# Decoder block with a routed feed-forward: the rows of the routed tiles turned by way of DRAM and VectorE in place of TensorE

## What is computed

```
x = x + ffn(layernorm(x))
probs  = softmax(h @ gate_w.T)            # h = layernorm(x), 2048 x 512
w, sel = top_k(probs, 2); w = w / sum(w)  # two of 8 experts for a token
out    = silu(h @ Gs.T) * (h @ Us.T) @ Ds.T                    # shared, 704 wide
out   += sum over chosen e: w_e * (silu(h @ G_e.T) * (h @ U_e.T)) @ D_e.T   # 352 wide
```

## Time and profile before

| | |
|---|---|
| median of 3 runs | 1596.42 us (1595.49 to 1596.97) |
| the profiled execution | 1598.12 us, of which 1596.4 us is its span |
| PE busy | 1563.7 us (98%) |
| DVE busy | 1030.9 us (65%) |
| ACT busy | 584.1 us (37%) |
| POOL busy | 448.0 us (28%) |
| TensorE clock granted | 0.997 of full speed on average |
| moved by DMA | 345.37 MB, mean 216 GB/s |

### The profile page before, as it was taken

One profiled execution on the slowest core, in us unless ns is written; L12 is line 12 of the kernel. 1 busy time (PEld: TensorE's weight loads), 2 busy tenths in 40 slices (PEclk: granted clock), 3 DMA queues, 4 the chain that ended last, 5 costly groups with the idle time before them and its releaser, 6 DMA issues.

```text
span 1596.4 us, 24261 instructions
## 1 busy us (share of the span) xinstructions
PE 1563.7 (98%) x8012; PEld 1352.6 (85%) x8013; DVE 1030.9 (65%) x2219; ACT 584.1 (37%) x997; POOL 448.0 (28%) x378
## 2 busy tenths in 40 slices
PE   7999999999999999999999999999999999999996
PEld 5888888888888888888888887788999989999995
DVE  4798767788777788777787778655663582222221
ACT  4454443434434334434334334333111312333332
POOL 3445332234123234222233221102200003333342
PEclk9999999999999999999999999999999999999998
DMA  8886564677676786776686776564621026778753
GB/s 290 282 305 211 184 219 146 237 279 260 256 268 226 261 303 238 257 282 224 243 312 248 297 303 241 165 209 157 239 94 54 7 105 211 235 201 267 211 87 40
DMA packets 97601, 345.37 MB, mean 216 GB/s; under 512 B 10144, under 2 KB 24992, under 8 KB 92000
## 3 DMA queue, kind: packets, MB, share of 16 engines
q1 hardware_dynamic: 84480, 306.33, 52.7%
q0 software_dynamic: 13024, 37.79, 10.1%
HBM read 224.03 MB, written 120.05 MB: 216 GB/s over the span
## 4 chain that ended last, share of the span: by engine, by line
PE 90%; DVE 5%; DMA 2%; POOL 1%; issue 1%; ACT 1%; SPq 0%; POOLq 0%; DVEq 0%; ACTq 0%
PE bank L360 29%; PE bank L362 28%; PE bank L361 28%; PE bank L1912 1%; PE bank L2029 1%; DMA wqk_raw<-wqk_in 1%; DMA wqk<-wqk_parts 1%; POOL store L633 0%; DVE resid L1235 0%; PE bank L1702 0%; DMA wv_raw<-wv_in 0%; DMA rows<-x_rows,ids_e 0%; POOL wqk L633 0%; PE bank L1986 0%; DVE place_hot L1591 0%
## 5 line engine op out<-in xcount | busy, mean ns | idle before, releaser
L674 POOL TENSOR_TENSOR probs<-probs,causal 128x256 f32<-128x256 f32 x126 | 90.5, 739 | 412.5 <-ACT probs L852 412.5
L360 PE MATMUL bank<-store,wqk 128*128 128x512 f32 x512 | 201.8, 394 | 0.3 <-DMA wqk<-wqk_parts 0.3
L362 PE MATMUL bank<-store,wqk 128*128 128x512 f32 x512 | 202.1, 395 | 0.0
L361 PE MATMUL bank<-store,wqk 128*128 128x512 f32 x512 | 201.8, 394 | 0.0
L1235 DVE SCALAR_TENSOR_TENSOR resid<-bank,factor,resid 128x512 f32<-128x512 f32 x256 | 189.4, 741 | 1.2 <-PE bank L362 1.1
L633 POOL TENSOR_TENSOR pre_split<-pre_raw,pre_split 128x1528 fp32r<-128x1528 f32 x34 | 120.6, 3548 | 140.9 <-ACT pre_split L814 140.9
L850 ACT ACTIVATE probs<-bank 128x512 f32<-128x512 f32 x189 | 85.8, 528 | 131.1 <-PE bank L362 131.1
L362 PEld LDWEIGHTS bank<-store,wqk 128*128 128x128 f32 x512 | 96.0, 188 | 22.9
L1229 DVE TENSOR_TENSOR q_lo<-bank,q_hi 128x512 fp32r<-128x512 f32 x64 | 44.3, 692 | 108.2 <-ACT q_hi L897 108.1
L361 PEld LDWEIGHTS bank<-store,wqk 128*128 128x128 f32 x512 | 96.0, 188 | 20.8
L360 PEld LDWEIGHTS bank<-store,wqk 128*128 128x128 f32 x512 | 96.0, 188 | 20.5 <-DMA wqk<-wqk_parts 0.8
(11 more groups left out here) (333 smaller groups left out, 3927.1 us busy)
## 6 DMA issues: line engine op xcount, KB each, us to landing
pre_parts<-pre_split SPq DMA_DIRECT2D x34, 1528.0 KB, 6.7
wqk<-wqk_parts SPq DMA_DIRECT2D x96, 512.0 KB, 4.6
pre_raw<-pre SPq DMA_DIRECT2D x34, 764.0 KB, 7.7
store<-wv_parts SPq DMA_DIRECT2D x12, 2048.0 KB, 9.0
wo<-wo_parts SPq DMA_DIRECT2D x48, 512.0 KB, 8.8
expert_w<-pre_parts SPq DMA_DIRECT2D x8, 2816.0 KB, 11.9
wqk_parts<-wqk SPq DMA_DIRECT2D x16, 1024.0 KB, 5.0
expert_w<-pre_parts SPq DMA_DIRECT2D x8, 1536.0 KB, 8.9
```

The lines of the kernel that those rows point to most:

```text
L360: nc.tensor.matmul(out_ap, a_hi, b_hi, start=first, stop=False)
L361: nc.tensor.matmul(out_ap, a_hi, b_lo, start=False, stop=False)
L362: return nc.tensor.matmul(out_ap, a_lo, b_hi, start=False, stop=last)
L674: nc.gpsimd.tensor_tensor(diagonal, diagonal, causal[:, :, :], ALU.mult).then_inc(S["masked"], 1)
```

## The change

From tile 2 on, PE no longer transposes the rows of routed tiles. After the gather, ACT stores the tile's 128 rows from `rows[g % 4]` to a new DRAM tensor `es` (`store_row_e`, semaphore `e_put`), waits for the landing, and loads the tile back with `load_turned`, four DMAs of 64 KB in pieces of 512 bytes, into `x3_early[4 + g % 4]` (`load_row_e`, semaphore `e_turned`). DVE turns its blocks into bank 4 (`turn_rows_e`). ACT's step g has, at its end, the load of tile g + 3 and the store of tile g + 4; before step 0 ACT stores tiles 2 and 3 and loads tile 2. DVE's turn of tile g + 2 stands at the end of its step g. POOL's gather g waits for the store of tile g - 4 in place of PE's transposes. Tiles 0 and 1 are still turned by PE. SP's wait for a new expert's gate and up weights is put on `e_up` in place of `e_xT_ready`, for the same tile.

```diff
+        es = nc.dram_tensor("es", (ETILES * P, D), F32, kind="Internal").ap()
...
-        E_ROWS, E_AHEAD = 4, 6
+        E_AHEAD = 6
+        def e_turn(g):
+
+            return len(range(g % E_ROWS, g + 1, E_ROWS)) - (g % E_ROWS < 2)
+
...
-        def load_turned(tile, source, done):
+        def load_turned(tile, source, done, engine=nc.sync):
 
             for r in range(QUADS):
-                nc.sync.dma_start(tile[r * BLOCK:(r + 1) * BLOCK, :].rearrange("x (a q) -> x a q", a=QUADS),
+                engine.dma_start(tile[r * BLOCK:(r + 1) * BLOCK, :].rearrange("x (a q) -> x a q", a=QUADS),
                                   source[:, r * P:(r + 1) * P].rearrange("(a x) q -> x a q", x=BLOCK)).then_inc(done, 16)
...
-                for part, used, lo, n in (("up", "e_xT_ready", 0, UP), ("down", "e_aT_ready", UP, DOWN)):
+                for part, used, lo, n in (("up", "e_up", 0, UP), ("down", "e_aT_ready", UP, DOWN)):
                     if e:
                         sp.wait_ge(S[f"{part}_loaded"], 16 * e)
                     if e >= 2:
-                        sp.wait_ge(S[used], tiles_before + 1)
+                        sp.wait_ge(S[used], tiles_before if part == "up" else tiles_before + 1)
...
-                if g >= E_ROWS:
+                if E_ROWS <= g < E_ROWS + 2:
                     pool.wait_ge(S["e_xT_ready"], g - E_ROWS + 1)
+                elif g >= E_ROWS:
+                    pool.wait_ge(S[f"e_put{g % E_ROWS}"], 16 * e_turn(g - E_ROWS))
...
+            def store_row_e(g):
+                act.wait_ge(S[f"e_row{g % 2}"], 16 * (g // 2) + 16)
+                nc.scalar.dma_start(es[g * P:(g + 1) * P], rows[:, g % E_ROWS, :]).then_inc(S[f"e_put{g % E_ROWS}"], 16)
+
+            def load_row_e(g):
+                act.wait_ge(S[f"e_put{g % E_ROWS}"], 16 * e_turn(g))
+                if g >= 2 + E_ROWS:
+                    act.wait_ge(S["e_xT_ready"], g - E_ROWS + 1)
+                load_turned(x3_early[:, E_ROWS + g % E_ROWS, :], es[g * P:(g + 1) * P], S[f"e_turned{g % E_ROWS}"], nc.scalar)
+
...
                     aT_high_last("e")
                     y_copy_e(g - 1)
+                if g + 3 < ETILES:
+                    load_row_e(g + 3)
+                if g + 4 < ETILES:
+                    store_row_e(g + 4)
...
             xT_high("e", 0)
+            store_row_e(2)
+            store_row_e(3)
+            load_row_e(2)
             for g in range(ETILES):
                 step_e(g)
...
+            def turn_rows_e(g):
+                dve.wait_ge(S["e_xT_lo"], g)
+                dve.wait_ge(S[f"e_turned{g % E_ROWS}"], 16 * QUADS * e_turn(g))
+                turn(x3_early[:, E_ROWS + g % E_ROWS, :]).then_inc(S["e_xT_ready"], 1)
...
                 step("e", g, first=g == 0, last=g == ETILES - 1)
+                if g + 2 < ETILES:
+                    turn_rows_e(g + 2)
...
                     p = place(g - 1)
-                    transpose_rows_e(i, j + 1)
                     e_down(g - 1, p, second, lambda: following.append(place(g + 1)))
...
             last = ETILES - 1
-            transpose_rows_e(last // 4, last % 4)
```

More of the change, by code:

```diff
@@ L248, in build @@
         xs_out = nc.dram_tensor("xs_out", (XTILES * P, D), F32, kind="Internal").ap()
+        es = nc.dram_tensor("es", (ETILES * P, D), F32, kind="Internal").ap()
         x3_rows = nc.dram_tensor("x3_rows", (T + P, D), F32, kind="Internal").ap()
+        E_ROWS = 4
         names = """x_tile0 x_tile1 x_tile2 x_tile3 x_loaded const_ready ln_eps ln_rstd xn_ready xr_ready x3_ready xnT_ready xnT_hi_done xnT_lo_done
@@ L264, in build @@
         """ + " ".join(f"{ph}_{n}" for ph in "xse" for n in ("xT_ready", "xT_hi", "xT_lo", "up", "silu", "act", "aT_ready", "aT_hi", "aT_lo", "y", "y_out"))
-        names += " " + " ".join(f"{n}{j}" for n in ("x_row", "e_row", "x_y_stored") for j in range(2))
+        names += " " + " ".join(f"{n}{j}" for n in ("x_row", "e_row", "x_y_stored") for j in range(2)) + " " + " ".join(f"e_{n}{j}" for n in ("put", "turned") for j in range(E_ROWS))
         S = {n: sem(n) for n in names.split()}
@@ L2024, in e_down, with transpose_rows_e @@
                                for part in (2 * UP, 2 * UP + DOWN)], second, between, to, parts)
-            def transpose_rows_e(i, j):
-                pe.wait_ge(S[f"e_row{j % 2}"], 32 * i + 16 * (j // 2) + 16)
+            def transpose_rows_e(g):
+                pe.wait_ge(S[f"e_row{g}"], 16)
                 for k in range(KC):
-                    last = nc.tensor.transpose(bank[XT][:, k * P:k * P + P], every(rows[:, j % 4, :], k), ident[:, :])
+                    last = nc.tensor.transpose(bank[XT][:, k * P:k * P + P], every(rows[:, g, :], k), ident[:, :])
                 last.then_inc(S["e_xT_ready"], 1)
@@ L2047, in first_rows_e @@
                 pe.wait_ge(S["s_y_out"], TILES - 1)
-                transpose_rows_e(0, 0)
+                transpose_rows_e(0)
             def first_up_e():
@@ L2052, in first_up_e @@
                 e_up(0, place(0), first=True)
-                transpose_rows_e(0, 1)
+                transpose_rows_e(1)
             pe.wait_ge(S["sh_zeroed"], 1)
```

## The result

The changed kernel takes 1654.22 us (median of 4 runs, 1653.13 to 1654.97), the kernel before, on the same chip, 1596.16. The ratio is 1.0361, 95% interval 1.0347 to 1.0375: slower by 58 us. The prediction was 1604.4 us with a range to 1619, so the change is slower, as was forecast, but by seven times as much.

The account below looks back on a forecast made before the run. PE was taken as the bound: -17.4 us of transposes and +7.0 at the start gave -10.4. With DMA engines (+7.5) or POOL's additions (+9.3) setting the pace, about +8 was forecast: 1604.4 us, range 1586 to 1619.

Parts of the forecast that it names:

- PE's step: Routed stage on PE: without four transposes a step falls from 6.74 to 6.27 us, -17.4 us over 37 tiles.
- DVE's turn: On DVE, one turn per tile of 1.10 us, hidden in idle time with 1.3 us left, costed at nothing.
- the two budgets: DMA engine time, +7.5 us, and POOL's chain of additions, +9.3 us, both with the start, meeting at about +8 us.
- the start: Before ACT's first silu: early stores, a load and the silu table delay it from 1321.59 to 1328.6, +7.0 us.
- ACT's issues: On ACT, five DMA issues a step at 0.32 us each, 1.6 us, fitting into its free time.
- ACT's wait for the store: On ACT before the load: a store issued some 4.7 us earlier lands after 2.1 us, early enough.
- DVE's wait for the turned load: On DVE before its turn: 1.3 us are left, only a load landing later than that delays DVE and PE; costed at nothing.
- Rival C: ACT stopped under weight loads: turned load needs 11 us, has about 7, 4 us lost at each of six, 1618 to 1630; chance 0.12.
- the sentence on queues taken in turn: At weight loads, each of 32 load pieces per DMA engine waits for one long weight packet, 15 us in all.
- The budget of DMA engine time: In six weight-load cycles the DMA engines need 28.1 us against 27.0 now and set the pace; +7.5 us with the start.
- The chain of POOL's additions: POOL's serial adds take 249.9 of 255.2 us, plus 0.2 us new delay each (7.6 us); +9.3 us with the start.

Follow-up runs that it names:

- nostore: Changed kernel with PE turning tiles 0 to 3 and no stores; loads read plain rows already in DRAM (wrong rows): 1637.10 us, ratio 1.0248.
- wide: Changed kernel with the tile loaded back as 128 plain rows of 2048 bytes, not 512 pieces of 512 bytes: 1637.97 us, ratio 1.0255.
- traffic_two: traffic with the additions of even and odd tiles in two chains on two tensors: 1594.72 us, ratio 0.9991.
- traffic: Kernel before, PE still turning, with the same stores and loads added but nobody waiting for the loaded tile: 1620.43 us, ratio 1.0138.
- nostore_deep: nostore with the load of tile g + 5 issued in step g, three steps before it is needed: 1609.63 us, ratio 1.0082.
- deep_two: Changed kernel with PE turning tiles 0 to 3, gather 8, store 6, load 4 tiles ahead, additions in two chains: 1613.51 us, ratio 1.0108.
- nostore_deep_two: nostore_deep with the additions in two chains (odd tiles' additions leave the result): 1576.96 us, ratio 0.9876.

## Why the prediction was wrong

**Right: PE's step. The sign was luck.** 6.27 us was forecast, 6.2 to 6.3 measured. DVE's turn (1.09 us) is hidden wherever the load is in time, as said. But without the two budgets the forecast's own sum was -10.4 us, and neither budget is what made this kernel slower (below).

**Nearly right: the start.** +7.0 forecast, +8.7 measured in the first silu, all three items being there (stores, load, the table behind the wait): the store of tile 2 landed 5.8 us after its issue at 1321.32, where 4 was taken, and the loads could be issued only at 1327.12. What it was worth in the time, 12.2 us, was more.

```profile
1321.32 4.07 ACTq L983 DMA_DIRECT2D es<-rows  x2
1327.12 1.86 ACTq L379 DMA_DIRECT2D x_early<-es  x4
1329.02 1.28 ACT L995 ACT_TABLE_LOAD   x1 [13.27 <-DMA rows<-x_rows,ids_e]
```

**Mis-sized, harmless: ACT's issues.** 0.32 us each were taken from SP. On ACT the four of a load took 1.76 us and the store 0.44, 2.2 us in all instead of 1.6; PE's pace of 6.25 us held.

**The step that failed: two landings beside a weight load, put at nothing.** One is ACT's wait for the store: it "lands after 2.1 us where it has the engines nearly to itself", "which is early enough". The other is DVE's wait for the turned load: "1.3 us are left and I cost it at nothing". The view of the store's line gives the landing of all 37:

```profile
DMA to landing us min/median/max: 2.2/4.2/15.2
```

Even the median is twice what was taken, and beside the weights the store took up to 15.2 us and the turned load 14.6. In place of the nothing that was put down stand 62.3 us at the six weight loads. The load's landing is enough for a long step: without the store 57.6 us stay (nostore). The store's alone was not run, but where the load was less late (wide) ACT's waits kept the long steps. The row for it was at hand, a gather at 10.6 us, and the forecast used the other one.

**Rival C was what happened, at 2.6 times its price.** It gave 4 us a weight load (needs 11, has 7); it was 10.4. The load's landing was up to 14.6 us, in nostore 15.0 to 16.0, and not 11; the sentence on queues taken in turn had 15 us. I carried the gather's 10.6 into the sum instead, though a gather fetches 128 rows of 2048 bytes and the load 512 pieces. And after the gap comes a second loss, the clock, below. C's chance of 0.12 was too low for a case that two rows spoke for.

**The forecast's own reasons: one false, one true but not reached.** The budget of DMA engine time (28.1 us a cycle) had the bytes right: in traffic_two the share rose by 0.25 over 150 us, 1.7 us for each of some 22 tiles, which was the forecast's term. Its conclusion, "That can't fit", is refuted: the share of 1.01 went with an unbroken pace of 27.0 us a cycle, so a sum of busy shares near 1 is no bound by itself. The chain of POOL's additions is a real bound behind the first. In the changed kernel it hardly shows, since POOL waits for ACT there. Its size was off: I took 0.2 us of new delay an addition; in traffic it is up to (277.6 - 249.9) / 38 = 0.73, in nostore_deep, with half of the bytes, up to (267.6 - 249.9) / 38 = 0.47 (up to, since PE and ACT still set some of these intervals). For traffic the bound of 0.9 was nearer. The mechanism was expected as a steady small delay; in fact it comes in lumps, at a weight load, where the second addition also starts late (8.6 us for 5.7).

So the 58 us, in the order in which the runs took things away: the start 12.2; the stores with their waits and bytes 4.9; the load's lateness 27.5 (1637.10 to 1609.63); the chain of additions 32.7 (to 1576.96); and against these 20.4 us that PE's shorter step and the second chain are worth (1597.38 to 1576.96). These causes overlap, so the order sets their shares: the chain's 32.7 us show only once the loads are in time, and no addition held up the changed kernel itself. They come to 56.9 us by construction; the kernel before itself differs by 1.2 us between the sets of runs. What stays open is how deep_two's 36.6 us over nostore_deep_two divide: 12.3 are at tile 8, whose store has one step only, the rest between the store's landing, its bytes and the row buffers. More row buffers weren't tried.

## What to carry to other kernels

Price the landing of a new transfer that someone waits for by the worst stretch of the trace, with the big load beside it, and ask how many steps ahead it is issued; the median (2.1 us here) says nothing about that stretch (15). Then look for the serial chain that is almost as long as the critical one: here by the prediction's estimate the additions needed 249.9 of 255.2 us, so that no saving on PE could be worth more than 5.3 us, while the new bytes alone cost 23 (traffic). A trade of 0.47 us of engine time for 512 KB of DMA traffic a tile needs both checks.

## What the hardware showed unexpectedly

After a gap of 9 us PE runs at a lower clock once it works again. Windows of the changed kernel (columns as above), over the gap, the step behind it, and the next:

```profile
1370.00:1380.00 10.00, 2.12 (x10) 1.40 (x8) 1.09 (x1) 0.00 (x0) 2.55 (x2) 0.72 0.88 278
1380.01:1387.61 7.60, 6.19 (x29) 5.73 (x29) 2.93 (x5) 2.02 (x6) 2.56 (x2) 0.70 0.69 169
1387.61:1393.90 6.29, 6.29 (x38) 5.84 (x37) 2.90 (x5) 2.02 (x6) 2.57 (x2) 1.00 0.35 73
```

The granted clock is 0.70 in the step behind the gap, a mix of the two levels (1.2 and 2.4 GHz), and full in the next. In PE's timeline the matmuls start 0.29 us apart at first and 0.16 us apart 2 us later:

```profile
1382.77 0.49 PE L367 MATMUL bank<-expert_w,xT_hi 128*128 x1
1383.06 0.49 PE L368 MATMUL bank<-expert_w,xT_lo 128*128 x1
...
1385.07 0.32 PE L367 MATMUL bank<-expert_w,xT_hi 128*128 x1
1385.23 0.32 PE L368 MATMUL bank<-expert_w,xT_lo 128*128 x1
```

The interval of 7.6 us is not all clock: PE idles for its first 1.1 us, and the nine matmuls of the down product had run ahead of the gap. The same work at both levels is a better measure, the transposes of the activations and the 24 matmuls of the gate and up products, up to the first of the down product, behind the gap (1381.15, above) and two steps later:

```profile
1387.38 0.39 PE L366 MATMUL bank<-expert_w,aT_hi 128*128 x1
...
1395.77 0.49 PE L1944 MATMUL bank<-ident,act_sb 128*128 128x128 f32 x3
...
1399.92 0.39 PE L366 MATMUL bank<-expert_w,aT_hi 128*128 x1
```

They take 6.23 us and 4.15 us. Of the 2.08 between them PE waits 0.27 for DVE's low part, so a stall of 9 us costs some 1.8 us more behind it through the clock.
